# A bf16 product with a cast behind it, and a bf16 scan result, in the recurrence of a Hawk block between two half FFNs

## The reference

```python
x = x + 0.5 * ffn(layernorm(x))
x = x + hawk(layernorm(x))
x = x + 0.5 * ffn(layernorm(x))

def ffn(x):  return relu(x @ w1 + b1) @ w2 + b2          # 1024 -> 4096 -> 1024
def hawk(x):
    gate, xa = split(x @ w_in.T)                          # 2 x 1024
    xc = causal_depthwise_conv(xa, w_conv, 4 taps) + b_conv
    forget, inp = split(xc @ w_gates.T + b_gates)
    alpha = exp(-8 * softplus(forget_base) * sigmoid(forget))
    beta = sqrt(1 - alpha**2 + 1e-6)
    u = beta * sigmoid(inp) * xc
    h[t] = alpha[t] * h[t-1] + u[t]                       # along the sequence
    return (gelu(gate) * h) @ w_out.T
```

## Time and profile before

| what | us |
|---|---|
| median of 2 runs | 7014.59 |
| the two runs | 6724.73 and 7304.44 |
| the profiled execution | 6737.94 |
| its span (slowest core, core 3) | 6736.4 |
| the other cores' spans | 6678.6 to 6719.6 |

### The profile page before, as it was taken

The page is one execution under the profiler, slowest core; times in us unless marked ns, Lnnn a source line. Parts: engine busy times, 40 slices in busy tenths (PEclk is TensorE's granted clock), DMA queues, the critical chain, the costliest instruction groups (busy, mean ns, idle before and its releaser), DMA issues.

```text
span 6736.4 us, 62420 instructions; the slowest of 8 cores (6678.6 to 6736.4 us)
## 1 busy us (share of the span) xinstructions
PE 5206.5 (77%) x22272; PEld 2211.8 (33%) x22272; DVE 2096.8 (31%) x3781; ACT 1556.6 (23%) x2347; POOL 413.3 (6%) x411
## 2 busy tenths in 40 slices
PE   5956789567895678956789568895688956888669
PEld 2422334223342233422334223342233422333224
DVE  2254222542225421254212542125421244122441
ACT  1132121321213212132121321113211231212311
POOL 0011000110001100011000110001100011000110
PEclk9978899788997889978899788997889977899779
DMA  5597222012220122201222012220122101221011
GB/s 100 87 119 120 75 75 88 26 50 75 75 88 25 50 75 75 88 26 50 75 80 83 25 50 75 88 75 25 50 75 100 63 25 50 75 100 63 36 39 51
DMA packets 159821, 450.75 MB, mean 67 GB/s; under 512 B 3040, under 2 KB 3040, under 8 KB 158688
## 3 DMA queue, kind: packets, MB, share of 16 engines
q1 hardware_dynamic: 149104, 392.23, 17.4%
q0 software_dynamic: 10416, 54.53, 6.2%
HBM read 467.72 MB, written 60.82 MB: 78 GB/s over the span
## 4 chain that ended last, share of the span: by engine, by line
PE 67%; DVE 14%; DMA 6%; issue 5%; ACT 3%; another core or an unknown queue 2%; POOL 1%; DVEq 0%; ACTq 0%; SPq 0%; POOLq 0%
PE ps L462 26%; PE ps L448 24%; PE ps L500 3%; DVE xc_t L524 3%; PE ps L629 3%; PE ps L405 3%; PE ps L550 3%; PE ps L543 3%; DMA wslot<-w_s 2%; DVE arenaC L401 2%; PE ps L396 2%; DVE arenaC L577 2%; DVE arenaC L428 2%; DMA x_t<-x 2%
## 5 line engine op out<-in xcount | busy, mean ns | idle before, releaser
L448 PE MATMUL ps<-arenaB,wslot 128*128 128x512 bf16 x8192 | 1870.8, 389 | 121.1 <-DVE arenaB L431 121.1
L462 PE MATMUL ps<-arenaA,wslot 128*128 128x512 bf16 x8192 | 1791.1, 381 | 34.3 <-DMA wslot<-w_s 34.3
L468 DVE SCALAR_TENSOR_TENSOR x_t<-ps,x_t 128x512 f32<-128x512 f32 x512 | 353.9, 691 | 2953.0 <-PE ps L462 2953.0
L448 PEld LDWEIGHTS ps<-arenaB,wslot 128*128 128x128 bf16 x8192 | 814.3, 100 | 1170.5 <-issue 253.9
L454 ACT ACTIVATE arenaA<-ps,b_t 128x512 bf16<-128x512 f32 x1024 | 703.7, 687 | 2063.1 <-PE ps L448 2063.1
L462 PEld LDWEIGHTS ps<-arenaA,wslot 128*128 128x128 bf16 x8192 | 804.3, 98 | 1011.8 <-issue 54.4
L396 PE MATMUL ps<-arenaC,ones_t 128*128 128x512 bf16 x384 | 158.9, 499 | 615.8 <-DVE arenaC L392 615.8
L500 PE MATMUL ps<-arenaB,wslot 128*128 128x512 bf16 x2048 | 486.8, 394 | 112.0 <-DVE arenaB L431 70.9
L613 POOL TENSOR_TENSOR arenaC<-arenaC 128x512 f32<-128x512 f32 x128 | 191.2, 1494 | 5553.4 <-ACT arenaC L610 5496.5
L543 PE MATMUL ps<-xc_t,wslot 128*128 128x512 bf16 x1024 | 261.5, 401 | 264.2 <-ACT arenaB L554 248.0
L414 ACT ACTIVATE arenaC<-ps,eps_t 128x512 f32<-128x512 f32 x48 | 33.0, 688 | 1670.8 <-PE ps L405 1670.8
(11 more groups left out here) (62 smaller groups left out, 2168.8 us busy)
## 6 DMA issues: line engine op xcount, KB each, us to landing
wslot<-w_s SPq DMA_DIRECT2D x60, 4096.0 KB, 16.8
x_t<-x SPq DMA_DIRECT2D x16, 2048.0 KB, 10.1
xout<-x_t SPq DMA_DIRECT2D x16, 2048.0 KB, 7.3
wslot<-win_s SPq DMA_DIRECT2D x7, 4096.0 KB, 15.5
wslot<-wg_s SPq DMA_DIRECT2D x7, 4096.0 KB, 15.7
wslot<-w POOLq DMA_DIRECT2D x4, 4096.0 KB, 53.2
wslot<-wo_s SPq DMA_DIRECT2D x7, 2048.0 KB, 9.8
w_s<-w POOLq DMA_DIRECT2D x2, 4096.0 KB, 73.6
```

The costliest lines, as they stand in the source:

```text
L448: e.matmul(ps[b][:], l, r, start=st, stop=sp),
L462: e.matmul(ps[b][:], l, r, start=st, stop=sp),
L468: e.scalar_tensor_tensor(xs, ps[b][:], 0.5, xs, ALU.mult, ALU.add),
```

## The change

hh_t and hc_t become bf16. The product of line 600 is written as bf16 to a new buffer ub_t, and a new copy on VectorE turns it into the f32 u_t, from which all goes on as before. ub_t stands at 10 KB in arenaC, where the second half of hh_t was; tb_t moves from 8 KB to 0 and from key C4 to C0. The keys of si_t and xb_t are renamed from C6.. to CS0.., and ub_t has the keys C6 and C7.

```diff
@@ arenaC
         ("u_t", [P, 2, TS], F32, 4 * KB),
-        ("hh_t", [P, 2, TS], F32, 8 * KB),
+        ("hh_t", [P, 2, TS], BF16, 8 * KB),
+        ("ub_t", [P, 2, TS], BF16, 10 * KB),
...
+        ("tb_t", [P, TS], BF16, 0),
...
-        ("tb_t", [P, TS], BF16, 8 * KB),
@@
-    hc_t = sb("hc_t", [P, KC], F32)
+    hc_t = sb("hc_t", [P, KC], BF16)
@@ ln_cast_chunk, ln_sq_chunk, ln_finish, h2_g_block, h2_chains: the same renaming at each use
-                  reads=("x:%d" % s,), writes=("C%d" % (6 + c),))
+                  reads=("x:%d" % s,), writes=("CS%d" % c,))
@@ ln_finish
             prog.comp("vector", lambda e, c=c: e.tensor_tensor(tb_t[:], xb_t[:, c, :], meanb_t[:], ALU.subtract),
-                      reads=("C%d" % (6 + c), "C3"), writes=("C4",))
+                      reads=("CS%d" % c, "C3"), writes=("C0",))
             prog.comp("vector",
                       lambda e, c=c, o=off: e.tensor_tensor(xn_t[:, c, o:o + TS], tb_t[:], rstdb_t[:], ALU.mult),
-                      reads=("C4", "C3"), writes=("B%d" % (2 * c + s),))
+                      reads=("C0", "C3"), writes=("B%d" % (2 * c + s),))
@@ h2_chains
             prog.comp("vector",
                       lambda e, c=c, pp=pp, o=off: e.tensor_tensor(
-                          u_t[:, pp, :], si_t[:, c, :], xc_t[:, c, o:o + TS], ALU.mult),
-                      reads=("C%d" % (6 + c), "xc:%d:%d" % (c, s)), writes=("C%d" % (2 + pp),))
+                          ub_t[:, pp, :], si_t[:, c, :], xc_t[:, c, o:o + TS], ALU.mult),
+                      reads=("CS%d" % c, "xc:%d:%d" % (c, s)), writes=("C%d" % (6 + pp),))
+            prog.comp("vector",
+                      lambda e, pp=pp: e.tensor_copy(u_t[:, pp, :], ub_t[:, pp, :]),
+                      reads=("C%d" % (6 + pp),), writes=("C%d" % (2 + pp),))
```

More of the change, by code:

```diff
@@ L262, in build_nc @@
         C["meanf_t"], C["ex2_t"], C["meanb_t"], C["rstdb_t"], C["tb_t"])
-    q_t, u_t, hh_t, si_t = (C["q_t"], C["u_t"], C["hh_t"], C["si_t"])
+    q_t, u_t, hh_t, ub_t, si_t = (C["q_t"], C["u_t"], C["hh_t"], C["ub_t"], C["si_t"])
     xa_t, y_t = Dv["xa_t"], Dv["y_t"]
@@ L396, in ln_cast_chunk @@
                   e.matmul(ps[6][:], ones_t[:], b, start=st, stop=sp),
-                  reads=("ones", "C%d" % (6 + c)), writes=("ps6",))
+                  reads=("ones", "CS%d" % c), writes=("ps6",))
     def ln_sq_chunk(s, c):
@@ L401, in ln_sq_chunk @@
                   lambda e, a=x2b_t[:, c % 2, :], b=xb_t[:, c, :]: e.tensor_tensor(a, b, b, ALU.mult),
-                  reads=("C%d" % (6 + c),), writes=("C0",))
+                  reads=("CS%d" % c,), writes=("C0",))
         prog.comp("tensor",
@@ L562, in h2_g_block @@
                           bias=bg2_t[:, KC + c:KC + c + 1]),
-                      reads=("ps%d" % bankI, "bg2"), writes=("C%d" % (6 + c),))
+                      reads=("ps%d" % bankI, "bg2"), writes=("CS%d" % c,))
             prog.comp("scalar",
@@ L597, in h2_chains @@
                           si_t[:, c, :], si_t[:, c, :], 0.5, 0.5, ALU.mult, ALU.add),
-                      reads=("C%d" % (6 + c),), writes=("C%d" % (6 + c),))
+                      reads=("CS%d" % c,), writes=("CS%d" % c,))
             prog.comp("vector",
                       lambda e, c=c, pp=pp, o=off: e.tensor_tensor(
-                          u_t[:, pp, :], si_t[:, c, :], xc_t[:, c, o:o + TS], ALU.mult),
-                      reads=("C%d" % (6 + c), "xc:%d:%d" % (c, s)), writes=("C%d" % (2 + pp),))
+                          ub_t[:, pp, :], si_t[:, c, :], xc_t[:, c, o:o + TS], ALU.mult),
[3 more added lines that the diff above has]
+                      reads=("C%d" % (6 + pp),), writes=("C%d" % (2 + pp),))
             prog.comp("vector",
```

## The result

The change makes the kernel 0.33% slower: the ratio of its times to those of before is 1.0033, with a 95% interval of 1.0020 to 1.0045, on 6726 us 22 us (13 to 30). The profiled execution took 6737.44 us, with a span of 6735.9 us. Before it was 6737.94 and 6736.4: on these two executions the difference does not show. The ratio comes from the undisturbed ones among 35 runs of before and 37 of the change; in the others, one half of the chip or both showed a lower clock. Of before these are 20, which lie between 6705.86 and 6730.33 us, so the profiled execution of before was a long one.

A forecast was written before the change was run, and what follows sets the result against it. The port VectorE and GpSimd share was taken to bound the h2 chains. Laid-out turns gave +8 us, plain lengths +8 to +27 less 3; +12 was taken on 6737.94, giving 6750 us (+0.2%), range 6695 to 6840.

The forecast's parts named there:

- the layout of the turns in the second chain: Second h2 chain, port turns laid out instruction by instruction: period 4.68 us against 4.74, -0.06 us an iteration.
- the rule that what waits finishes early: VectorE and GpSimd on the shared port: a blocked instruction finishes about 0.15 us earlier than its own duration would say.
- The plain sum of lengths: Both chains, 104 exposed iterations at +0.08 to +0.26 us: +8 to +27 us, less 3 for GpSimd's gate product.
- the dependence gap: VectorE, cast reading the product just ahead of it: 0.18 us extra, in which GpSimd can have the port.
- The product and the cast: VectorE in the chains: bf16 product 0.42 us instead of 0.69, added cast 0.41 us, bounds 0.26 to 0.69.
- Rival C: VectorE in the chains: product doesn't speed up, or cast takes 0.69 us; +28 us on top, 6778 us; chance 0.13.
- The first chain: First h2 chain, turns laid out: period 4.59 us against 4.41, +0.18 an iteration, 1.1 us a macro step.
- TensorE's wait: First gate matmuls behind the first chain: wait for ScalarE's activation goes from 248 to 257 us.
- The start of the second chain: Undisturbed start of c=0 in the second chain: +0.26 us a macro step.
- rival B: GpSimd's gate product takes 0.6 us with all operands bf16: faster, -57 us, total 6693 us; chance 0.08.
- Rival A: Port turns fall badly once in each iteration: 1.26 us longer, +131 us, total 6869 us; chance 0.09.
- Rival D: Chains get faster as order settles into short steps of 3.7 us: -90 us, total 6648 us; chance 0.04.

The follow-up runs named there:

- E3: The changed kernel with the cast one place later, behind the operation on q; ratio to before 1.0000 (0.9977 to 1.0023).
- E5: The changed kernel with the cast done twice in a row; ratio to before 1.0114 (1.0092 to 1.0135).
- E10: The changed kernel with the next chunk's operation on si between product and cast, q behind the cast; ratio to before 0.9990 (0.9971 to 1.0010).
- E11: As E10, but with the operation on q ahead of the cast; ratio to before 0.9983 (0.9964 to 1.0003).
- E7: As E4 (no cast), with the gate product y moved from GpSimd to VectorE; ratio to before 0.9918 (0.9897 to 0.9940).
- E9: As E8, with the operation 0.5 si + 0.5 moved from VectorE to ScalarE; ratio to before 0.9843 (0.9822 to 0.9864).
- E4: The changed kernel without the cast, GpSimd's product with q reading the bf16 product itself; ratio to before 0.9950 (0.9930 to 0.9969).
- E8: As E7, with the product with q moved from GpSimd to VectorE too; ratio to before 0.9889 (0.9871 to 0.9907).

## Where the prediction held, and the step that failed

The direction, the place and the mechanism held: the kernel got slower, in the chains, by the cast and by turns at the port. The size did not: +12 us was forecast, a little over half of the 22 (13 to 30) that the ratio says. The step that failed is the layout of the turns in the second chain.

- **The second chain** was laid out to a period of 4.68 us, -0.06 against before, in all -0.4 us. It came to 4.89, +0.15, and from the first q to the last +0.95. The two wrong terms are in the rows shown above. The layout had line 613 (now 617) wait for the operation on si until 2.11 and end at 3.16, by the rule that what waits finishes early by 0.15 to 0.2 us. But it waited for only 0.13 us, took its full 1.26 and ended at 1407.14, which is 3.26 after line 608. The same rule was used for the gate product behind line 582 (now 583): the layout let it end 1.04 us after the product on VectorE, and it took its full 1.14. Each is 0.1 us, 0.21 an iteration. The rows show this; no run tests the rule by itself.
- **The choice of +12.** The plain sum of lengths gave +8 to +27, less 3. The lower end came from giving the dependence gap of 0.18 us away to GpSimd. The upper end, 24, is near the 22 measured; +12 was taken since the layout stood at +8.
- **The base.** The 12 us were added to the 6737.94 of one execution, which lies above all 20 runs of before that the ratio rests on; their mean is 6718. That the forecast total of 6750 lies only 13 us over the middle of the changed kernel's runs (6737) says nothing for it: the base was 20 us high and the difference 10 us low.
- **The product and the cast.** 0.42 was forecast for the product, and 0.424 is its shortest; 0.41 for the cast, and its shortest is 0.426 right behind the product and 0.411 behind an independent instruction (E3). Neither bound of the cast's price was near. Rival C falls with this.
- **The dependence gap** counts in part to wholly. The distance from start to start is 0.53 us with it and 0.34 without, so it is 0.19. E5's second cast adds 0.46 us to the period of the first chain and 0.53 to that of the second: more than half of the gap, and all of it. E10 parts two such pairs, 2 x 0.19 = 0.38 us, and takes away 0.25 and 0.15.
- **The first chain** was laid out turn by turn to 4.59 us, and it came to 4.61; from the first to the last q the sum was to be +1.1 us, and it was +1.23. TensorE's wait was to be 257 us, and it was 258.3. This is in part luck: 2.0 of the 10.3 us come from the first macro step, whose chain is longer by that much.
- **Where the time is lost within a chain** is less even than a period says. The step from c=1 to c=2 grew by 1.13 us in the first chain (3.17 to 4.30) and by 1.16 in the second (4.39 to 5.55). The five steps behind it add up to 23.94 before and 24.04 after, and to 24.68 and 24.46. Before, the steps alternate between long and short, so a whole chain also depends on which kind it ends on.
- **The start of the second chain** was forecast at +0.26 us; from TensorE's last matmul to the first q it went from 1.70 to 1.96, +0.26.
- **The sum again, with what was measured:** 1.23 + 0.95 + 0.26 = 2.44 us a macro step, 8 x 2.44 = 20 us, inside the 13 to 30 of the ratio.
- **GpSimd** lost 0.008 us on the gate product by its shortest use (1.151 to 1.143) and 0.015 by the median (1.160 to 1.145), where 0.03 was taken; rival B, 0.6 us, is out. B's own total of 6693 also lay just below the range that was said to hold it. The scan's 1.27 stayed, as forecast; its mean rose from 1517 to 1565 ns while its shortest stayed at 1269.
- **Rival A**, an iteration longer by 1.26 us, did not happen in each iteration: what is lost ahead of q is largely won behind it. A loss of about that size is seen once in a chain, at c=2. What E10 and E11 add is that the position of q hardly moves the period. **Rival D** did not happen either, and E7 to E9 show what it takes to get to 3.7 us: GpSimd's work, or most of it, has to leave the port.

## What to carry to other kernels

Where two engines take turns at one port and the sum of their own lengths is close to the period, count what each instruction adds from start to start, and its dependence gap in part to wholly (here 0.12 to 0.19 of 0.19 us for one more cast), since there is little slack that hides it. A cast put in to make one product cheaper (0.27 us) loses by its own length (0.41 here); let the next reader take the narrow type, or part the two with an independent instruction. And when the port is full, a product is worth more on the engine that does it in 0.42 us and not in 1.15, even though that engine looks like the busy one.

## What the runs showed that was not expected

- GpSimd's product of two 512-column tiles takes 1.26 us all in f32, 1.151 with one bf16 input, whether its output is f32 (E4) or bf16 (before), and 1.143 with all three in bf16 (each the shortest use). The first narrow input saves 0.11 us, the second next to nothing.
- Taking work from GpSimd and giving it to the busier VectorE shortened the chains: E8's are 11.1 us a macro step shorter than before, of which 4.7 came with E4 and 6.4 with the two products that moved. VectorE's busy time in the profile had been waiting in large part: 1244 ns for a product that takes 691.
- Line 617 started 0.13 us before the operation on si had ended and showed its full 1.26, so this wait cost nothing. In E3 it started 0.27 us before the scan's end and took 1.33, which ends 1.06 after the scan: the 0.2 us by which a blocked instruction seems to finish early had to be waited for first. This is read from rows and wasn't tested by itself.
